# Attention on one core: the mask of four head pairs moved from TensorE to GpSimd, the row scaling moved from GpSimd to VectorE

## The reference, cut to what matters

```python
x = _ln(src) * (1.0 + scale) + shift            # scale, shift: one row per batch
q = (x @ Wq + bq).reshape(B, S, 16, 32).transpose(0, 2, 1, 3)   # k, v alike
scores = jnp.einsum('bhqd,bhkd->bhqk', q / math.sqrt(32), k)
scores = scores + attention_bias                # (8, 16, 512, 512)
scores = jnp.where(src_mask, -jnp.inf, scores.astype(jnp.float32))
probs = jax.nn.softmax(scores, axis=-1).astype(v.dtype)
ctx = jnp.einsum('bhqk,bhkd->bhqd', probs, v)
x = x + (ctx @ Wo + bo)
```

## Time and profile before

| | us |
|---|---|
| median of 3 runs | 2872.56 (2868.95 to 2876.88) |
| the profiled execution, its time | 2875.56 |
| the profiled execution, its span | 2873.8 |
| TensorE busy | 2659.9 (93%) |
| VectorE busy | 1771.7 (62%) |
| GpSimd busy | 1026.4 (36%) |
| ScalarE busy | 951.0 (33%) |

### The profile page before, as it was taken

The page is one execution under the profiler, slowest core; times in us unless marked ns, Lnnn a source line. Parts: engine busy times, 40 slices in busy tenths (PEclk is TensorE's granted clock), DMA queues, the critical chain, the costliest instruction groups (busy, mean ns, idle before and its releaser), DMA issues. The chain is left out here.

```text
span 2873.8 us, 48156 instructions
## 1 busy us (share of the span) xinstructions
PE 2659.9 (93%) x17072; PEld 2040.2 (71%) x17088; DVE 1771.7 (62%) x3500; ACT 951.0 (33%) x2032; POOL 1026.4 (36%) x741
## 2 busy tenths in 40 slices
PE   6975999999999999699999999996999999999997
PEld 2434777777777777477888888885777777777775
DVE  8965777777777777565444444433665665566544
ACT  1114666666666666311111111111112111211212
POOL 1004787777777775531111001102332222222210
PEclk9997999999999999899999999998999999999998
DMA  4325554554545545331100000001543343233311
GB/s 156 113 82 168 166 188 144 184 170 162 189 144 183 191 140 164 114 103 45 30 1 31 30 31 1 30 15 61 165 121 103 99 120 108 93 116 117 98 46 37
DMA packets 212640, 306.13 MB, mean 107 GB/s; under 512 B 14266, under 2 KB 93178, under 8 KB 209722
## 3 DMA queue, kind: packets, MB, share of 16 engines
q1 hardware_dynamic: 210682, 299.88, 32.3%
q0 software_dynamic: 1728, 3.16, 0.5%
HBM read 268.94 MB, written 34.05 MB: 105 GB/s over the span
## 5 line engine op out<-in xcount | busy, mean ns | idle before, releaser
L783 POOL TENSOR_TENSOR at_bias<-at_bias,at_mask 128x1024 f32<-128x1024 f32 x224 | 480.0, 2147 | 248.0 <-DMA at_bias<-in_fside_Bx16xSxS 246.7
L1148 DVE CUSTOM_DVE_ANT_0 at_bias<-at_bias,at_bank_score 128x512 f32<-128x512 f32 x512 | 337.7, 680 | 183.2 <-PE at_bank_score L1014 137.8
L875 ACT ACTIVATE at_y<-at_bias,at_nmax 128x512 f32<-128x512 f32 x512 | 366.5, 717 | 20.3 <-DVE at_nmax L1148 20.3
L1542 POOL TENSOR_SCALAR expert_WH<-expert_stage 128x1024 fp32r<-128x1024 f32 x128 | 164.3, 1284 | 516.4 <-PE expert_bank_out L98 315.9
L1021 PE MATMUL at_bank_probT<-at_ident,at_y 128*128 128x128 f32 x2048 | 313.6, 280 | 6.6 <-ACT at_y L875 6.6
L1876 DVE CAST ff_gH<-ff_g 128x512 fp32r<-128x512 f32 x128 | 70.0, 547 | 387.1 <-ACT ff_g L1615 386.8
L1021 PEld LDWEIGHTS at_bank_probT<-at_ident,at_y 128*128 128x128 f32 x2048 | 228.6, 141 | 94.7 <-issue 66.2
L1615 ACT ACTIVATE expert_g<-expert_bank_hid,expert_b1c 128x512 f32<-128x512 f32 x128 | 88.3, 690 | 623.7 <-PE expert_bank_hid L98 623.7
L1615 ACT ACTIVATE ff_g<-ff_bank_hid,ff_b1c 128x512 f32<-128x512 f32 x128 | 88.2, 689 | 610.1 <-PE ff_bank_hid L98 610.1
L883 ACT ACTIVATE at_probT<-at_bank_probT 128x512 f32<-128x512 f32 x256 | 153.0, 598 | 272.0 <-PE at_bank_probT L1021 159.7
L1876 DVE CAST expert_gH<-expert_g 128x512 fp32r<-128x512 f32 x128 | 68.5, 535 | 259.7 <-ACT expert_g L1615 259.7
(11 more groups left out here) (327 smaller groups left out, 5657.8 us busy)
## 6 DMA issues: line engine op xcount, KB each, us to landing
at_bias<-in_fside_Bx16xSxS SPq DMA_DIRECT2D x256, 512.0 KB, 3.5
expert_stage<-in_L_cond_Wi SPq DMA_DIRECT2D x128, 256.0 KB, 2.9
expert_stage<-in_L_cond_Wo SPq DMA_DIRECT2D x128, 256.0 KB, 3.0
st_f<-in_x SPq DMA_DIRECT2D x8, 1024.0 KB, 7.0
x_after_layer<-st_y SPq DMA_DIRECT2D x8, 1024.0 KB, 4.8
at_x<-x_after_layer SPq DMA_DIRECT2D x32, 256.0 KB, 4.6
x_after_attention<-at_x SPq DMA_DIRECT2D x32, 256.0 KB, 2.3
ff_x<-x_after_attention SPq DMA_DIRECT2D x32, 256.0 KB, 4.0
```

Source lines behind the costliest of these rows:

```text
L783: pool.tensor_tensor(bias[i % NB][:, :, :], bias[i % NB][:, :, :], mask[:, i // 2 % R, :].unsqueeze(1).to_broadcast([P, 2, S]), ALU.add).t ...
L875: act.activation(prob[u % 2][:, :], bias[u // 2 % NB][:, u % 2, :], ACT.Exp, scale=-1.0, bias=nmax[:, u % 4:u % 4 + 1], accum_out=sums[:, ...
L1148: dve.tensor_tensor_reduce(t, t, pS[u % HC][:, :], -1.0, 3.0e38, ALU.add, ALU.min, nmax[:, u % 4:u % 4 + 1]).then_inc(s_max, 1)
L1542: pool.tensor_scalar(WH[:, f, :], stage[f % 2][:, :], 1.0, 0.0, ALU.mult, ALU.add).then_inc(s_wh, 1)
```

## The change

All 32 pairs get their mask on GpSimd, and the products with the identity are gone. The multiplication of the next batch's rows by the scale goes to VectorE, at steps 29 to 32 behind that step's sum. The addition of the shift stays on GpSimd, at steps 31 to 34 instead of 33 to 36. Counts and waits follow.

```diff
-        ON_PE = range(18, 22)
-        NM = NP - len(ON_PE)
-        ident16 = sb("ident16", [P, P], BF16)
...
-        s_first = sem("first_rows_scaled")
+        s_scaled = sem("rows_scaled")
...
 (SP, load_scale_shift)
-                wait_count(sp, s_ln, n * (2 * R))
+                wait_count(sp, s_ln, n * R)
...
 (GpSimd)
-            def scale_shift(n, slot, k):
-                step, r = divmod(k, R)
+            def add_shift(n, slot, r):
                 xr = x[slot][:, r, :]
-                if step == 0:
-                    if r == 0:
-                        pool.wait_ge(s_ab, n * 32 + 32)
-                    pool.wait_ge(s_xhat, n * R + r + 1)
-                    pool.tensor_tensor(xr, xr, scale[:, :], ALU.mult).then_inc(s_ln, 1)
-                if step == 1:
-                    pool.wait_ge(s_ln, n * (2 * R) + r + 1)
-                    pool.tensor_tensor(xr, xr, shift[:, :], ALU.add).then_inc(s_ln, 1)
+                pool.wait_ge(s_scaled, n * R + r + 1)
+                pool.tensor_tensor(xr, xr, shift[:, :], ALU.add).then_inc(s_ln, 1)
...
 (make_mask)
-                    pool.wait_ge(s_bm, n * NM)
-                    pool.wait_ge(s_qk, (n - 1) * NG + max(ON_PE) // 2 + 1)
+                    pool.wait_ge(s_bm, n * NP)
...
-            scale_shift_at = (29, 30, 31, 32, 33, 34, 35, 36)
-            pool.tensor_copy(ident16[:, :], ident[:, :]).then_inc(s_cm, 1)
+            shift_at = (31, 32, 33, 34)
...
-                    if cur and u % 2 == 0 and i not in ON_PE and (nxt or m is n):
+                    if cur and u % 2 == 0 and (nxt or m is n):
                         add_mask(m, i)
...
 (TensorE, scores)
-                if pair == min(ON_PE):
-                    pe.wait_ge(s_mask, (n + g // NG) * 2 + 2)
-                masked = [pair + j // 2 in ON_PE for j in range(HC)]
-                for j in range(HC):
-                    if masked[j]:
-                        pe.matmul(pS[j][:, :], ident16[:, :], mask[:, r, :], start=True, stop=False)
...
 (VectorE)
+            def apply_scale(n, slot, r):
+                if r == 0:
+                    dve.wait_ge(s_ab, n * 32 + 32)
+                dve.wait_ge(s_xhat, n * R + r + 1)
+                dve.tensor_tensor(x[slot][:, r, :], x[slot][:, r, :], scale[:, :], ALU.mult).then_inc(s_scaled, 1)
...
 (sum_scores)
-                    if i in ON_PE:
-                        dve.wait_ge(s_bias[i % NB], m * (NP // NB * 16) + 16 * (i // NB + 1))
-                    else:
-                        dve.wait_ge(s_bm, m * NM + sum(k not in ON_PE for k in range(i + 1)))
+                    dve.wait_ge(s_bm, m * NP + i + 1)
...
 (body, behind sum_scores, row_stats and mean_var of the step)
+                    if nxt and 29 <= u < 29 + R:
+                        apply_scale(n + 1, 1 - slot, u - 29)
```

More of the change, by code:

```diff
@@ L784, in add_mask @@
                                    ALU.add).then_inc(s_bm, 1)
-            scale_shift_at = (29, 30, 31, 32, 33, 34, 35, 36)
-            pool.wait_ge(s_id, 2)
-            pool.sem_inc(s_passed, 1)
-            pool.tensor_copy(ident16[:, :], ident[:, :]).then_inc(s_cm, 1)
-            pool.wait_ge(s_cm, 2)
+            shift_at = (31, 32, 33, 34)
+            pool.wait_ge(s_cm, 1)
             power(0)
@@ L794, in _ @@
             for i in range(3):
-                if i not in ON_PE:
-                    add_mask(0, i)
+                add_mask(0, i)
             pool.wait_ge(s_const, 64)
@@ L825, in body @@
                         pool.tensor_tensor(cL[k][:, :], pv[k], f32(cH[k][:, :]), ALU.subtract).then_inc(s_cl, 1)
-                    if nxt and u in scale_shift_at:
-                        scale_shift(n + 1, 1 - slot, scale_shift_at.index(u))
+                    if nxt and u in shift_at:
+                        add_shift(n + 1, 1 - slot, shift_at.index(u))
                     if nxt and u in (50, 52, 54, 56):
@@ L957, in transpose_x @@
                 if m == 0:
-                    pe.wait_ge(s_ln, (n + 1) * (2 * R))
+                    pe.wait_ge(s_ln, (n + 1) * R)
                 for r in range(R):
@@ L1002, in scores @@
                 wait_count(pe, s_cc, n * NG + g - 2)
-                pair = 2 * g % NP
-                if pair == min(ON_PE):
-                    pe.wait_ge(s_mask, (n + g // NG) * 2 + 2)
-                masked = [pair + j // 2 in ON_PE for j in range(HC)]
-                for j in range(HC):
-                    if masked[j]:
-                        pe.matmul(pS[j][:, :], ident16[:, :], mask[:, r, :], start=True, stop=False)
                 parts = ((qH[c % 2], kH[c % 2]), (qL[c % 2], kH[c % 2]), (qH[c % 2], kL[c % 2]))
@@ L1013, in scores @@
                         rows = slice(j * HD, (j + 1) * HD)
-                        mm = pe.matmul(pS[j][:, :], q[rows, r * P:(r + 1) * P], key[rows, :], start=k == 0 and not masked[j], stop=k == 2)
+                        mm = pe.matmul(pS[j][:, :], q[rows, r * P:(r + 1) * P], key[rows, :], start=k == 0, stop=k == 2)
                 mm.then_inc(s_qk, 1)
@@ L1047, in _ @@
             transpose_v(0, 0, first_bank("v", 0))
-            pe.wait_ge(s_cm, 2)
             scores(0, 0)
@@ L1186, in _ @@
             mean_var(0)
-            dve.wait_ge(s_ab, 32)
             for r in range(R):
-                dve.wait_ge(s_xhat, r + 1)
-                dve.tensor_tensor(x[0][:, r, :], x[0][:, r, :], scale[:, :], ALU.mult).then_inc(s_first, 1)
+                apply_scale(0, 0, r)
             for r in range(R):
-                dve.wait_ge(s_first, r + 1)
-                dve.tensor_tensor(x[0][:, r, :], x[0][:, r, :], shift[:, :], ALU.add).then_inc(s_ln, 2)
+                dve.wait_ge(s_scaled, r + 1)
+                dve.tensor_tensor(x[0][:, r, :], x[0][:, r, :], shift[:, :], ALU.add).then_inc(s_ln, 1)
             weights_low(0)
```

## The result

| | us |
|---|---|
| before, median of 8 runs | 2873.53 (2868.95 to 2879.19) |
| changed, median of 8 runs | 2884.78 (2882.69 to 2889.92) |
| ratio, 95% interval | 1.0045 (1.0036 to 1.0054) |
| span of the profiled execution | 2886.3 (before 2873.8) |

The changed kernel is slower by 0.45%: 12.9 us by the ratio, 11.3 between the two medians, 12.5 between the two spans. The forecast had 5.8 us, rival 1 had 17.8.

What follows compares the result with a forecast made beforehand. TensorE was taken to bound the kernel. Seven batches of group 9's delay (1.4 or 2.55 us) less 0.9, and 1.8 off in the eighth, gave +1.7 or +9.8; the middle, +5.8, made 2881.4 us (median 2878.4), range 2866 to 2892.

Steps and rivals of the forecast that it cites:

- rival 1: At step 31 GpSimd wins the shared SBUF read before VectorE's second scaling: +17.8 us, 2890.4 us; chance 0.33.
- What bounds: In the attention batches TensorE bounds, with only 1 us of slack per 116.6 us batch, so its delays reach the end.
- Masks off TensorE, 14.4 us: Score groups 9 and 10 lose four mask products each, 0.90 us a group: 16 groups, 14.4 us, the most to gain.
- Masks onto GpSimd cost nothing: Steps 29 to 36: four more adds a batch (8.6 us) replace four scalings (5.2 us); GpSimd keeps up, costing nothing.
- Scaling 1 behind mask 18: VectorE's first scaling, asked for at 669.04, waits until pair 18's mask add releases the read at 670.0; about 1.65 us.
- Plain time of the scalings, +0.3 us at group 9: Three scalings delay the sum of unit 35 on VectorE; without exclusion score group 9 starts at 675.30 instead of 674.99.
- Exclusion: A VectorE operation on two SBUF tiles and a GpSimd operation wait for each other's whole operation; some shifts near 1.9 us.
- The dead heat at scaling 2: VectorE's second scaling and GpSimd's mask add of pair 19 both reach for the shared read at 671.8.
- VectorE first: VectorE's second scaling gets the read before pair 19's mask add; group 9 then +1.4 or +2.55 us late.
- The sum: Whole kernel: +5.8 us on the profiled span, 2881.4 us, median 2878.4; forecast "no change, on the slow side".
- Its own signs: Batch period 117.1 to 118.3 us, TensorE idle some 2.3 to 3.4 us a batch; a scaling above 2.5 us means rival 1.
- Middle of two cases: Third scaling slips between GpSimd operations (+1.7 us over all batches) or misses (+9.8 us); +5.8 us taken between them.

Runs made afterwards that it cites:

- e7: Changed kernel, but VectorE scales only two row tiles (steps 29, 33), GpSimd the other two (steps 29, 31), shifts at 32, 33, 34, 36; 0.9946 of the kernel before.
- e2: Kernel before with only the masks moved: all 32 mask adds on GpSimd, scaling and shift still there; 2862.52 us, 0.9966 of the kernel before.
- e1: Changed kernel with a one-SBUF-input statistics operation in place of VectorE's scaling from the second batch on; 2865.92 us, 0.9972 of the kernel before.
- e4: Changed kernel plus a 0.2 us GpSimd memset ahead of pair 19's mask add at step 32; 2873.55 us, 1.0004 of the kernel before.
- e5: Changed kernel with VectorE's scalings at steps 29, 33, 35, 37 and GpSimd's shifts at 31, 34, 36, 38; 2872.31 us, 0.9991 of the kernel before.

## Why the prediction came out as it did

- *What bounds.* Right. TensorE had no slack: each delay of it went into the period.
- *Masks off TensorE, 14.4 us.* Right: without a wait group 9 follows group 8 in 6.83 us instead of 7.72 and group 10 follows group 9 in 7.18 instead of 8.06. e7 keeps 12.3 of it.
- *Masks onto GpSimd cost nothing.* Right in the changed kernel, for the sums. With the scalings left on GpSimd it is wrong by the x transposes (e2), a case the prediction did not have to price.
- *Scaling 1 behind mask 18.* Right: 1.65 us were expected for its row, 1.52 to 1.79 measured in six batches and 2.48 in the last of the seven.
- *Plain time of the scalings, +0.3 us at group 9.* Right: it is 0.29 in e1, and the attention stretch has 5.7 us less, against the 6.0 of the sum.
- *Exclusion.* Right, shown by e1. The shifts that it makes longer took up to 1.74 us, where the prediction had some near 1.9.
- *The dead heat at scaling 2.* This is the step that failed. The forecast took "VectorE first". GpSimd was first in six batches of seven, by 0.02 or 0.03 us each time, where the sum had both at 671.8. Its own terms, not rounded, have mask 19 at 670.0 + 0.69 - 0.16 + 1.25 = 671.78 and scaling 2 at 670.0 + 3 x 0.60 = 671.80; that the sign agrees may be luck, since each term is rounded to 0.01 us or more. What the sum could have shown is that both paths start from the end of scaling 1, so that whichever is first in one batch is first in all where the bias has landed. The argument that a late landing of mask 19 would decide for VectorE was sound as a mechanism (batch 1) but was given too much weight: it came once. In five of the other six batches the bias had 3.6 to 3.8 us from its issue to mask 19, in the last 4.45, and that was enough. The price of losing was right: group 9 was to be 3.7 us late and was 3.69 to 3.84 late in five batches; +2.8 us a batch were computed, and the periods grew by 2.5 to 3.1 (to 119.2 to 119.6 from 116.6, and the first to 118.7 from 115.6).
- *The sum.* Six batches at 2.8, batch 1 at 0.5 and the eighth at -1.8 make 6 x 2.8 + 0.5 - 1.8 = +15.5 us; the attention stretch grew by 15.8, the span, with prologue and later layers a little shorter in this profile, by 12.5. The forecast's +5.8 us was about half of what came, and its "no change within 0.3%" fell by those six lost races. The range held because it had been drawn out to rival 1, which had a chance of 0.33 and is what happened in six batches; that the time of 2884.8 lies midway between the forecast's 2878.4 and rival 1's 2890.4 is due to the one late landing and to some 3 us less outside the attention stretch, neither of which the sum had. The case that the forecast was worked out for occurred in one batch of seven. Its own signs said so: a scaling of more than 2.5 us (2.66) was to be rival 1, the period of 119.5 lies above 117.1 to 118.3, and TensorE's idle time of 4.2 us above 2.3 to 3.4.
- *Middle of two cases.* I took the mean of slipping through and missing at scaling 3. In e4, where scaling 2 wins, scaling 3 slips through in all seven batches, so the better of the two would have been right there, and the forecast's single number belongs to no batch.

## What to carry to other kernels

An engine that looks half idle is not free at a given place: read which of its operations the bound engine waits for, and put the moved work behind that one, in the gap where it waits itself; then look for what is late because of it (in e5 the transposes). Moving work from GpSimd to VectorE with two SBUF inputs puts both on one read, so a cost shows as longer operations and not as waits; look for durations above the least one of their group. And where two engines reach for it at nearly the same moment, ask whether both run from one event: then a lead of 0.03 us repeats in every batch and is no chance. Don't average over the outcomes but change the order, so that the operation the bound engine depends on is first by a clear margin.

## What was not expected of the hardware

A 0.2 us operation added to the busier of two engines made the kernel 11 us faster (e4), since 0.03 us had decided between 0.68 and 2.66 us. An operation with one SBUF input of 512 elements, the statistics, was not held at all beside mask adds (687 ns in the median, 694 at most), while on the same engine a negation of 128x4 elements, with one SBUF input too, took 0.17 us in the prologue and 1.58 to 1.81 in six of the seven batches before (0.66 in the first, so not quite "in every batch"). Both read one SBUF tile; why the one is held and the other not was not tried. The Trainium skill, "SBUF — State Buffer" (Who interferes with whom), counts the one-input scalar operation (`tensor_scalar`, as the negation is) among those that can use both ports and so contend with GpSimd. These two rows fit that.
